# The mix stage of a four-layer convolution kernel: its first product's operand loaded three units ahead, and two rows of weights copied to PSUM

## What is computed

```
rel = nbhd_extract(coords, 7) - coords[:, :, None, :]
P   = relu(rel @ W1 + b1) @ W2 + b2
Wsm = softmax(P, axis=2)[0]                    # over the 49 neighbours
V   = nbhd_extract(x, 7)                       # 7 x 7 neighbourhoods, zero outside
out = einsum('nrc,bnrc->bnc', Wsm, V)
x   = x + out
```

## Time and profile before

| | us |
|---|---|
| median of the runs | 6821.06 |
| the profiled execution | 6821.58 |
| its span, first to last instruction | 6819.7 |
| VectorE busy | 5149.9 (76%) |
| GpSimd busy | 4754.8 (70%) |
| TensorE busy | 4541.4 (67%) |
| GpSimd, products with windows (L516), 160 | 463.2 |
| GpSimd, mask operations (L605), 28 | 74.7 |

### The profile page before, as it was taken

One profiled execution on the slowest core, in us unless ns is written; L12 is line 12 of the kernel. 1 busy time (PEld: TensorE's weight loads), 2 busy tenths in 40 slices (PEclk: granted clock), 3 DMA queues, 4 the chain that ended last, 5 costly groups with the idle time before them and its releaser, 6 DMA issues. The chain is left out here.

```text
span 6819.7 us, 55261 instructions
## 1 busy us (share of the span) xinstructions
PE 4541.4 (67%) x14990; PEld 2454.8 (36%) x14990; DVE 5149.9 (76%) x4038; ACT 2515.4 (37%) x3865; POOL 4754.8 (70%) x3364
## 2 busy tenths in 40 slices
PE   2755765576466546633325787878888787888887
PEld 1543552233323323422222343434333343443443
DVE  2855864367666766766655898989989898998998
ACT  0111110212111101200005565666666565666664
POOL 0744752277777777777754787878878787887887
PEclk8766777575566566555557999999999999999999
DMA  3533542334443543433323444444454444444443
GB/s 115 115 73 67 115 92 63 94 104 122 124 130 104 142 131 104 136 120 105 105 87 113 147 152 142 153 139 162 141 151 149 145 148 150 150 152 142 153 151 117
DMA packets 377421, 853.16 MB, mean 125 GB/s; under 512 B 194816, under 2 KB 237720, under 8 KB 372772
## 3 DMA queue, kind: packets, MB, share of 16 engines
q1 hardware_dynamic: 292420, 618.02, 30.6%
q0 software_dynamic: 84672, 231.32, 11.2%
HBM read 766.90 MB, written 56.48 MB: 121 GB/s over the span
## 5 line engine op out<-in xcount | busy, mean ns | idle before, releaser
L2016 POOL TENSOR_TENSOR ma_hc<-ma_h,ma_cc 128x784 f32<-128x784 f32 x1024 | 1885.7, 1849 | 631.9 <-DVE ma_h L1918 497.6
L797 POOL DMA_INDIRECT fl_quad<-table,fl_idx x1764 | 1694.5, 961 | 779.0 <-issue 536.7
L1573 PE MATMUL ma_bank<-ma_hc,ident 128*128 128x392 f32 x4096 | 1530.1, 496 | 76.2 <-POOL ma_hc L2016 76.2
L1918 DVE TENSOR_TENSOR_SCAN ma_h<-ma_da,ma_state,ma_bank 128x784 f32<-128x784 f32 x768 | 1417.5, 1846 | 165.6 <-POOL ma_hc L2016 67.6
L1791 ACT ACTIVATE ma_da<-ma_dt,ma_a_neg 128x784 f32<-128x784 f32 x1024 | 948.3, 943 | 496.3 <-DVE ma_h L1918 479.5
L952 DVE TENSOR_TENSOR fl_part<-fl_quad,fl_bank 128x2304 f32<-128x2304 f32 x196 | 500.5, 2554 | 741.2 <-DMA fl_quad<-table,fl_idx 740.9
L1906 DVE TENSOR_TENSOR ma_bank<-ma_dtu,ma_bank 128x784 f32<-128x784 f32 x1024 | 981.3, 958 | 38.3 <-PE ma_bank L1560 37.6
L1094 PE MATMUL fl_bank<-ident,fl_tap 128*128 128x128 f32 (+1 forms) x980 | 245.8, 414 | 989.7 <-DVE xres L969 929.1
L1573 PEld LDWEIGHTS ma_bank<-ma_hc,ident 128*128 128x128 f32 x4096 | 711.1, 191 | 506.5 <-POOL ma_hc L2016 80.2
L1560 PE MATMUL ma_bank<-ma_bc,ma_sel 96*128 96x512 bf16 (+1 forms) x2048 | 518.9, 335 | 442.4 <-DVE ma_h L1918 430.9
L960 DVE TENSOR_REDUCE fl_tap<-fl_part 128x576 f32<-128x2304 f32 x196 | 796.4, 4063 | 0.1
(11 more groups left out here) (217 smaller groups left out, 6166.2 us busy)
## 6 DMA issues: line engine op xcount, KB each, us to landing
ma_cc<-c_rows SPq DMA_DIRECT2D x512, 784.0 KB, 4.1
mx_win<-flat SPq DMA_DIRECT2D x64, 878.0 KB, 10.4
fl_quad<-table,fl_idx POOLq DMA_INDIRECT x1764, 2.7
table<-fl_xt SPq DMA_DIRECT2D x64, 392.0 KB
mx_mask<-in_c_mask SPq DMA_DIRECT2D x56, 294.0 KB, 4.3
ma_xs<-ma_x SPq DMA_DIRECT2D x64, 196.8 KB, 5.4
ma_xs<-ma_x SPq DMA_DIRECT2D x64, 196.5 KB, 5.8
mx_xf<-flat SPq DMA_DIRECT2D x8, 816.0 KB, 15.1
```

The costliest lines, as they stand in the source:

```text
L797: gp.indirect_dma_start(quad[i][:, kk, :], None, k["tables"][q], bass.IndirectOffsetOnAxis(ap=idx[i][:, kk:kk + 1], axis=0))\
L1573: ins = pe.matmul(ps_y[:, t, :], ident[:], hc[:, n % RH, at], start=False, stop=(n == DS - 1))
L1918: dve.tensor_tensor_scan(h[:, i % RH, :], da[:, i % RH, :], ps_bu[i % 2], before, ALU.mult, ALU.add).then_inc(scand, 1)
L2016: gp.tensor_tensor(hc[:, i % RH, :], h[:, i % RH, :], cc[:, i % (NGRP * GRP), :], ALU.mult)\
```

## The change

Two things change in `stage_mix`, and a third goes with them.

`rel` and `w1` get a third copy (69 partitions instead of 37). `load_unit` is split: `load_rel(U)` waits for the hidden product of U-3 only, `load_mask(U)` for the mask operation of U-2 as before. SyncE issues the first three `rel` of a group ahead, then `rel` of unit i+3 at step i, and the masks of unit i from i = 2 on.

ScalarE copies the two rows of weights that VectorE multiplies by, after the mask, into the PSUM tiles `hps` and `pps` (`lift`), which no product uses while the windows are worked on. VectorE reads them there (`held`), and waits for the copies before its first window. TensorE's first hidden product of the next group waits for the last of VectorE's multiplies (`vprod`).

`band` gets a semaphore of its own (`band_in`), for which TensorE waits before the transposes; it no longer counts among the constants.

```diff
         s = Space(nc, ctx, "mx")
-        w1 = s.sb("w1", [37, P])
+        w1 = s.sb("w1", [69, P])
         w2 = s.sb("w2", [P, P])
         b2 = s.sb("b2", [P, 1])
-        rel = s.sb("rel", [37, NJ * COL])
+        rel = s.sb("rel", [69, NJ * COL])
         mask = [s.sb(f"mask{i}", [P, NJ, KB, RC]) for i in range(2)]
...
         pps = s.ps("pps", [P, NJ, 512])
+        held = [ps[:].rearrange("p j n -> p (j n)")[:, 0:NJ * COL].rearrange("p (j n r) -> p j n r", j=NJ, n=KB)
+                for ps in (hps, pps)]
         tps = [s.ps(f"tps{i}", [P, 4, P]) for i in range(2)]
...
         zeroed = s.sem("zeroed")
-        rel_in = [s.sem(f"rel_in{i}") for i in range(2)]
+        rel_in = [s.sem(f"rel_in{i}") for i in range(3)]
         mask_in = [s.sem(f"mask_in{i}") for i in range(2)]
...
         win_in = [s.sem(f"win_in{i}") for i in range(2)]
-        vprod, gprod, reduced, kept = (s.sem(x) for x in ("vprod", "gprod", "reduced", "kept"))
-        pair_in, turned, placed, edged, restored, banded, scaled = (
-            s.sem(x) for x in ("pair_in", "turned", "placed", "edged", "restored", "banded", "scaled"))
+        vprod, gprod, reduced, kept, lifted = (
+            s.sem(x) for x in ("vprod", "gprod", "reduced", "kept", "lifted"))
+        pair_in, band_in, turned, placed, edged, restored, banded, scaled = (
+            s.sem(x) for x in ("pair_in", "band_in", "turned", "placed", "edged", "restored", "banded", "scaled"))
         stored = [s.sem(f"stored{i}") for i in range(2)]
...
         NV, NP = len(OWN), len(GP)
-        NCONST = 2 * 6 + 1
+        NCONST = 2 * 8
...
-            def load_unit(U):
+            def load_rel(U):
+                r = U % 3
+                sp.wait_ge(hidden, START + max(U - 2, 0))
+                sp.dma_start(rel[32 * r:32 * r + 5, :], k["c_rel"][U]).then_inc(rel_in[r], 16)
+            def load_mask(U):
                 r = U % 2
-                sp.wait_ge(hidden, START + max(U - 1, 0))
-                sp.dma_start(rel[32 * r:32 * r + 5, :], k["c_rel"][U]).then_inc(rel_in[r], 16)
                 sp.wait_ge(masked, START + max(U - 1, 0))
...
                 own = slice(h * CH, (h + 1) * CH)
-                for r in range(2):
+                for r in range(3):
                     sp.dma_start(w1[32 * r + 2 * h:32 * r + 2 * h + 2, own], k["W1"]).then_inc(consts, 16)
...
                 sp.dma_start(b2[own, :], k["b2"]).then_inc(consts, 16)
-            load_unit(0)
-            load_unit(1)
-            sp.dma_start(band[:].rearrange("p a b m -> p (a b m)"), k["c_band"]).then_inc(consts, 16)
+            for U in range(3):
+                load_rel(U)
+            for U in range(2):
+                load_mask(U)
+            sp.dma_start(band[:].rearrange("p a b m -> p (a b m)"), k["c_band"]).then_inc(band_in, 16)
             load_pair(0)
             for g in range(NG):
-                for i in range(2, KS):
-                    load_unit(KS * g + i)
+                for i in range(KS):
+                    if 3 <= i + 3 < KS:
+                        load_rel(KS * g + i + 3)
+                    if i >= 2:
+                        load_mask(KS * g + i)
                 if g < NG - 1:
...
                         load_window(g, slot, slot)
-                    load_unit(KS * (g + 1))
-                    load_unit(KS * (g + 1) + 1)
+                    for i in range(3):
+                        load_rel(KS * (g + 1) + i)
+                    for i in range(2):
+                        load_mask(KS * (g + 1) + i)
                     with sp.Fori(1, NB // 2) as bp:
...
             def hide(U):
-                r = U % 2
-                pe.wait_ge(rel_in[r], START + 16 * (U // 2 + 1))
+                r = U % 3
+                pe.wait_ge(rel_in[r], START + 16 * (U // 3 + 1))
                 pe.wait_ge(relued, START + U)
+                if U % KS == 0:
+                    pe.wait_ge(vprod, START + NV * NB * (U // KS))
                 for j in range(NJ):
...
             def uniform(g):
+                pe.wait_ge(band_in, START + 16)
                 pe.wait_ge(pair_in, START + 32 * (g + 1))
...
+            def lift(g):
+                for a, i in enumerate(OWN):
+                    act.wait_ge(masked, START + KS * g + i + 1)
+                    act.copy(held[a], wts[:, i]).then_inc(lifted, 1)
...
                     exponential(KS * g + i)
+                lift(g)
                 uniform(g)
-        def product(eng, out, slot, i):
-            w = win[slot][:]
+        def product(eng, out, slot, i, w):
+            v = win[slot][:]
             at = HALO + (i - KS // 2) * WD + JW[0] - KS // 2
-            src = bass.AP(w.tensor, w.offset + at, [list(w.ap[0]), [1, NJ], [SPAN, KB], [1, RC]])
-            return eng.tensor_tensor(out[:], src, wts[:, i], ALU.mult)
+            src = bass.AP(v.tensor, v.offset + at, [list(v.ap[0]), [1, NJ], [SPAN, KB], [1, RC]])
+            return eng.tensor_tensor(out[:], src, w, ALU.mult)
...
                 dve.wait_ge(masked, START + KS * (g + 1))
+                dve.wait_ge(lifted, START + len(OWN) * (g + 1))
                 with dve.Fori(0, NB // 2) as bp:
...
                             dve.wait_ge(reduced, freed(u, OWN[a]))
-                            product(dve, prodv[a], slot, OWN[a]).then_inc(vprod, 1)
+                            product(dve, prodv[a], slot, OWN[a], held[a]).then_inc(vprod, 1)
...
                             gp.wait_ge(reduced, freed(u, i))
-                            product(gp, prodg[a], slot, i).then_inc(gprod, 1)
+                            product(gp, prodg[a], slot, i, wts[:, i]).then_inc(gprod, 1)
```

## The result

| | before | after |
|---|---|---|
| median of 4 runs, us | 6822.37 (6818.94 to 6824.74) | 6540.15 (6535.08 to 6546.53) |
| the profiled execution, us | 6821.58 | 6535.08 |
| its span, us | 6819.7 | 6533.2 |
| last multiply of the mix stage, start in the span | 1049.78 | 760.3 |
| first load of the next stage | 1076.38 | 786.15 |

The ratio is 0.9587 [0.9571, 0.9604]. The forecast was 6531, 9 us too low. The next stage starts 290.2 us earlier where 290 had been worked out, so the miss lies outside the stage.

A forecast was written before the change was run, and what follows sets the result against it. VectorE and TensorE wait on a loop through GpSimd's mask and the late load of rel. The last seventh maximum gains 276 us and the tail 14, together 290: 6821.6 - 290 = 6531 us, range 6495 to 6585.

The forecast's parts named there:

- products start behind it: Start of a group's products: 16.45 us behind the seventh maximum, against 16.55 before.
- last stores behind it: Stage end: the last stores follow VectorE's end, with 14 us taken as gained behind the last seventh maximum.
- The bound: Mix stage units: the loop normalise, mask, SyncE, load of rel, two products set a cadence of 22.86 us.
- The cadence: Units with the operand three ahead: maxima 7.7 us apart, between VectorE's 6.75 and TensorE's 8.42.
- VectorE's end of the bounds, 6.75: Lower bound of the unit cadence: VectorE's own work alone, 6.6 us, with the starts 6.75.
- The start: Stage start, band out of the first wait: first hidden product at 74.9, 7.8 us earlier; first maximum at 89.0.
- The products: Windows, weights in PSUM: multiply 1.38 us, GpSimd sets the pace at 12.44 a window, phase 101.0 us.
- The group's end: TensorE waits for VectorE's last multiply; next maximum at +125.4 instead of 134.0, VectorE idling 6.5 us.
- The clock at 2.4 GHz throughout: Rival, TensorE in the units: full clock, VectorE's 6.75 sets the cadence; 6492 us, chance 0.12.
- the row: Profile row: TensorE's clock at 0.50 from 312 to 313, busy the whole microsecond, mid hidden product.
- The contention rival: Rival, products: VectorE and GpSimd hold each other up despite PSUM, windows stay 14.48 us; 6588 us, chance 0.08.
- The slow loads: Rival, window loads: 13.7 us each, two windows in 27.6, 6.6 more a group; 6557 us, chance 0.12.

The follow-up runs named there:

- e1_ahead_only: The changed kernel without its PSUM part: VectorE multiplies by weights in SBUF, ScalarE makes no copies, the operand stays three units ahead; 6574.72 us, ratio 0.9639.
- e2_psum_only: The kernel before with the PSUM part alone: copies, multiplies out of PSUM, wait for the last multiply; 6788.6 us, ratio 0.9953.
- e7_band_first: The changed kernel with band counted among the constants again, so TensorE waits for it before its first product; 6558.22 us, ratio 0.9612.
- e4_short_hidden: The changed kernel with the hidden product made for one of three column blocks, except in a group's first unit; 6514.69 us, ratio 0.9554.
- e5_score_by_block: The changed kernel with the score and VectorE's reading of it handed over block by block; 6524.31 us, ratio 0.9562.
- e11: The changed kernel with the score handed over by block and window loads waiting for the products, not VectorE's sums; 6512.8 us, ratio 0.9542.
- e3_copies_in_sbuf: The changed kernel with ScalarE's copies of the weights put into private SBUF tiles instead of PSUM; 6605.27 us, ratio 0.9687.
- e6_early_start: The changed kernel with windows 0 and 1 issued behind unit 3's masks and ScalarE's first copy before its last exponential; 6545.13 us, ratio 0.9592.
- e12_end_of_group: Against e11: ScalarE's first copy before its last exponential, the next group's first hidden product waiting for one multiply less; 6514.86 us, ratio 0.9548.
- e13: The changed kernel with four unread 128-row products behind each hidden product except a group's first; 6533.71 us, ratio 0.9574.

## Why the prediction was right

| step | predicted | measured |
|---|---|---|
| first hidden product; first maximum | 74.9; 89.0 | 73.67; 87.84 |
| cadence of the units | 7.7 | 7.86, 7.86, 7.86, 7.99 |
| seventh maximum | 135.2 | 135.00 |
| products start behind it | 16.45 | 15.6, 15.4, 16.3, 16.1 |
| multiply; GpSimd's time for a window | 1.38; 12.44 | 1.37; 12.21 |
| GpSimd's waits for late windows, first group | 1.44 | 3.1 |
| next first maximum | +125.4 | +123.6, +123.5, +125.1 |
| VectorE's gap there | 6.5 | 5.28, 5.30, 6.24 |
| last seventh maximum | 650.0 | 649.33 |
| last stores behind it | 123.5 | 124.0 |

**The bound.** That the loop through GpSimd and `rel` set the cadence, and not work, held: e1_ahead_only has that part and `band`'s and gains 248.3 of the 289.5 us, and e2_psum_only without them stays at 22.2 to 23.4. With `band`'s 12.7 of e7_band_first taken off, the operand alone is worth some 236.

**The cadence** was right in size and half right in reason. I had taken it between TensorE's 8.42 and VectorE's 6.75, as a choice between two engines. I had named the score's wait for VectorE, and not added the score to it. What holds most units is a chain over both, 3.64 of VectorE and then 4.3 of the score, since the score has one PSUM tile. The hidden product lies in VectorE's part, which e4_short_hidden showed; where it takes 4.28 and not 2.24, TensorE's own 8.43 stands instead. VectorE's end of the bounds, 6.75, isn't reached when that chain is opened either: in e5_score_by_block and e11 its own work takes 7.54, with 1.1 us more in a small step that is held until the mask operation ends.

**The start** came 1.2 us early in both places. `rel` was issued at 71.17, where 70.9 had been worked out, but the hidden product began 2.5 us later, not 4. e7_band_first takes `band`'s part back at 11.0 us: the whole of the 9.0 us between the first maxima of before and after is `band`'s place, and more.

**The products.** The hold-up is gone on both engines, and e3_copies_in_sbuf shows that it was the two operands in SBUF, not the shared tile. Two sizes in this step were off and cancel. A window takes GpSimd 12.21 and not 12.44, because I multiplied the median duration by five where starts lie 2.44 apart. And the loads made it wait 3.1 us in the first group, since the same windows are worked off sooner while the load takes as long. So 8 x 12.21 + 3.4 (0.27 us of waits beside the three) is 101.1 against the 101.0 forecast. The rule of the Trainium skill that I had cited ("SBUF — State Buffer", section "Who interferes with whom") holds here: a median of 1.37 in the multiplies with one operand in PSUM, and GpSimd at its own rate.

**The group's end.** The new wait of TensorE was foreseen with the 6.5 us that it gives back; it came to 5.28 to 6.24. The next maximum is 1.9, 1.9 and 0.3 us earlier than forecast: in the first two groups 0.7 because the last multiply ends at +111.1 and not at +111.8, and 1.2 because the products behind it take 12.4 us and not 13.6, as TensorE does the first of them partly at full rate. Two things are late there within about a microsecond of each other, the band products and the last multiply. Taking 1.0 to 1.4 us off both gave next to nothing (e6_early_start, e12_end_of_group), because the hidden product behind them then ran at the lower rate for longer; what decides when the clock falls there stays open.

**Luck in the middle.** The last seventh maximum came within 0.7 us of the forecast because errors cancel: the start 1.2 early, the 24 units 4.6 late in all (7.89 instead of 7.7), the three group ends 4.1 early.

**The last 9 us.** The profiled run gained 286.5 us, where its last multiply came 289.5 earlier: what lies behind it, the same code, took 5772.9 us against 5769.9. Over the kernels here that remainder varies by 16 us, so 3 us of it aren't explained by any step. The median is another 5 us above the profiled run. By this kernel's own spread of 11 us that is one run against another; its cause stays open.

**The rivals.** The clock at 2.4 GHz throughout would have given 6492: the granted 0.64 and the 12.4 us at 0.50 speak against it. The rule of the Trainium skill that I had set against the row ("TensorE: Matmul & The Clock Gate", section "What's actually happening") has the clock drop on idling and the busy array at 2.4 GHz. The traces agree in part: eight of nine falls came while TensorE was idle, and e11 is at 1.00 while busy in band products (236 to 240). They differ in the rest: the level stayed at 0.50 through 12.4 us of unbroken work, and in the kernel before it fell at 311.5, in a hidden product, with TensorE busy throughout from 308 on. The contention rival (6588) fell by the 1380 ns of the slowest multiply. The slow loads (13.7 each) fell by pairs of windows in 25.8, 25.4 and 25.2, where it needed 27.6.

## What to carry to other kernels

When an engine idles for a small load, follow the load's issue back through its queue: here it was queued behind loads that waited for another engine's work, and moving the issue ahead gave about four fifths of the gain. Between two engines that pass one buffer back and forth, add up the chain over both; neither engine's own sum is the cadence, and splitting the handover by blocks opens it. Before trimming the end of a stage, look for the second thing that is late there within a microsecond, and for what the work behind both will do: here a slower first product took back a microsecond won on both.

## What the runs showed of the hardware that was not expected

- A tensor_scalar of 24 columns, SBUF to SBUF, takes 0.24 us alone and up to 1.33 beside GpSimd's mask operation: it ends 0.02 to 0.04 us behind that operation's end in all 16 cases of e5, so it is held until then and not slowed. VectorE's maxima and shifts, which read PSUM, aren't held up by it. I had counted operands only. The Trainium skill, "SBUF — State Buffer", section "Who interferes with whom", also lists tensor_scalar among the operations that can enter a two-port mode and then contend with GpSimd; the trace agrees, with 1.32 against 0.24.
- Where two instructions contend, both get longer: in e3 VectorE's multiply goes from 1.38 to a median of 2.75, GpSimd's product from 2.49 to up to 3.69.
- TensorE's granted clock can fall to 0.50 while it is busy without a pause: at 311.5 of the kernel before, in a product over five rows, and at 97.25 and 104.0 of e13, in products over 128 rows behind one over five. It was 1.00 in 236 to 240 of e11 at the end of the band products. More products between the hidden ones raised the mean of the first group's units from 0.64 to 0.78.
- Small loads behind the windows' bytes on the same queue landed 16 to 17 us after their issue, 4.45 us too late for GpSimd, where masks had been in time in the changed kernel.
